# Splitting on GpSimd, and PSUM sums sorted by SyncE's DMAs, in a three-way attention loop

## The reference

```python
att = softmax(einsum('bthd,bshd->bhts', q * HD ** -0.5, k), axis=-1)
o = einsum('bhts,bshd->bthd', att, v)
```

## Time and profile before

| | us |
|---|---|
| median of 3 runs | 1794.24 |
| lowest, highest | 1793.36, 1794.6 |
| the profiled execution, by the same clock | 1795.07 |
| its span, first to last instruction | 1793.2 |
| TensorE matmuls, busy | 1589.7 (89%) |
| VectorE, busy | 1276.4 (71%) |
| ScalarE, busy | 1208.4 (67%) |
| GpSimd, busy | 697.1 (39%) |

### The profile page before, as it was taken

How to read it: one execution, slowest core, us unless ns; L and a number is a source line. 1 busy time by engine, 2 the same in 40 slices (tenths; PEclk the granted TensorE clock), 3 DMA queues, 4 the chain that set the end, 5 groups by cost and what they waited for, 6 DMA issues and landing times. The chain is left out here.

```text
span 1793.2 us, 36960 instructions
## 1 busy us (share of the span) xinstructions
PE 1589.7 (89%) x9638; PEld 728.6 (41%) x9638; DVE 1276.4 (71%) x3087; ACT 1208.4 (67%) x2377; POOL 697.1 (39%) x673
## 2 busy tenths in 40 slices
PE   3669947889999999999999999999999999855998
PEld 1217933333344343434434344334434343211665
DVE  6986856378787877878787787878787787452442
ACT  3325741757878778787878878787888878714333
POOL 7823441234344344344344334434434433221442
PEclk9559965889999999999999999999999999957999
DMA  2211125354564555465456456456455545030122
GB/s 51 73 44 37 47 54 71 42 80 62 63 77 65 66 71 77 53 78 73 56 71 78 65 60 85 59 64 77 64 67 71 76 50 72 2 36 26 58 60 58
DMA packets 132338, 109.25 MB, mean 61 GB/s; under 512 B 21824, under 2 KB 125248, under 8 KB 132288
## 3 DMA queue, kind: packets, MB, share of 16 engines
q1 hardware_dynamic: 130240, 104.44, 41.5%
q0 software_dynamic: 2048, 4.20, 0.9%
HBM read 19.26 MB, written 8.39 MB: 15 GB/s over the span
## 5 line engine op out<-in xcount | busy, mean ns | idle before, releaser
L1034 ACT ACTIVATE probs<-psum 128x512 f32<-128x512 f32 (+3 forms) x1536 | 737.8, 551 | 268.3 <-PE psum L1143 158.4
L915 DVE TENSOR_REDUCE mx_S<-psum 128x1 f32<-128x512 f32 x512 | 323.5, 684 | 74.6 <-PE psum L1128 72.7
L915 DVE TENSOR_REDUCE mx_C<-psum 128x1 f32<-128x512 f32 x512 | 317.5, 683 | 53.0 <-PE psum L1128 51.6
L915 DVE TENSOR_REDUCE mx_T<-psum 128x1 f32<-128x128 f32 (+3 forms) x512 | 240.6, 488 | 119.7 <-PE psum L1131 107.6
L847 POOL TENSOR_TENSOR rem_q<-f_q,parts_q 128x512 f32<-128x512 f32 x48 | 55.4, 1155 | 495.8 <-ACT parts_q L1020 479.2
L1128 PE MATMUL psum<-ks_S,qs_S 96*128 96x512 bf16 x512 | 201.7, 400 | 18.0 <-DMA ks_S<-parts_k 13.7
L1128 PE MATMUL psum<-ks_C,qs_C 96*128 96x512 bf16 x512 | 203.0, 398 | 12.4 <-DMA ks_C<-parts_k 7.3
L1143 PE MATMUL psum<-qs_C,ks_C 99*128 99x512 bf16 x512 | 193.6, 389 | 18.1 <-ACT probs L1034 11.5
L1143 PE MATMUL psum<-qs_S,ks_S 99*128 99x512 bf16 x512 | 195.9, 384 | 1.6 <-ACT probs L1034 0.9
L1128 PE MATMUL psum<-ks_T,qs_T 96*128 96x128 bf16 (+3 forms) x512 | 157.6, 310 | 7.4 <-DMA ks_T<-parts_k 6.0
L1143 PE MATMUL psum<-qs_T,ks_T 99*128 99x256 bf16 (+3 forms) x512 | 153.6, 302 | 7.6 <-ACT probs L1034 6.4
(11 more groups left out here) (188 smaller groups left out, 2702.3 us busy)
## 6 DMA issues: line engine op xcount, KB each, us to landing
qs_S<-parts_q SPq DMA_DIRECT2D x96, 128.0 KB, 4.2
ks_S<-parts_k SPq DMA_DIRECT2D x96, 128.0 KB, 6.8
qs_T<-parts_q SPq DMA_DIRECT2D x96, 128.0 KB, 4.4
ks_T<-parts_k SPq DMA_DIRECT2D x96, 128.0 KB, 6.8
qs_C<-parts_q SPq DMA_DIRECT2D x96, 128.0 KB, 4.4
ks_C<-parts_k SPq DMA_DIRECT2D x96, 128.0 KB, 6.8
w_in_S<-in_s_in SPq DMA_DIRECT2D x16, 257.0 KB, 2.7
w_in_T<-in_t_in SPq DMA_DIRECT2D x16, 257.0 KB, 2.7
```

Source lines behind the costliest of these rows:

```text
L915: nc.vector.tensor_reduce(mx[kind][:, n:n + 1], psum[:, ring_place(kind, b, n, RL), 0:last_key], AX_X, ALU.max)\
L1034: nc.scalar.activation(probs[:, n // 4 % 2, n % 4, t0:T], psum[:, LOGITS + ring_place(kind, b, n, RC), t0:T], ACT.Exp, scale=SCALE).then_i ...
```

## The change

Three things change in `attend`; the embedding stage and the MLP lose only the columns `low` and `high`.

1. GpSimd writes all parts. For queries, then for keys, it rounds high, subtracts, rounds middle, subtracts, where ScalarE did the two roundings; and it makes the three parts of the maxima (`split_maxima`, first in each slot), where VectorE did. The reduction itself negates, and VectorE only copies the transposed maxima out of `desk`.
2. After each group ScalarE copies the bank once, plainly, into `group_0` or `group_1`. SyncE sorts the 16-partition halves with DMAs of 32 KB, four to a call: first sums into `s_all` (end of the slot), second sums into `s_all`, second values over `group_0`'s sums. GpSimd's two additions and VectorE's shuffle go. The product now needs the second values landed, and ScalarE's copy into `group_0` at step 28 needs the product of the finishing unit (as `u_all` did).
3. SyncE's order in a slot: rows of maxima, weights, six query DMAs as their parts come, three DMAs of the keys' high part, second sums, three DMAs of the keys' middle and low parts, second values, and at the end first sums. The logarithm moves from step 21 to step 23 and reads `s_all`.

The diff of these places (indentation cut):

```diff
 TURN_AT, NEGATE_AT = 1, 1
 PROJECT_AT = (3, 7, 10)
-HIGH_AT, MIDDLE_AT = (4, 8), (9, 13)
+KEPT_AT = (4, 8)
 WEIGH_AT = 3
 VALUES_AT = 13
 GROUP_1_AT, GROUP_2_AT = 28, 12
-SWAP_AT, RECIP_AT = 17, 21
+RECIP_AT = 23
 OUTPUT_AT, KEEP_AT = 29, 31
 PROJECT_PARTS, OUTPUT_PARTS = (1, 1, 4), 2
 LAG = 8
...
     e = sp.value_load(expert[0:1, bass.ds(2 * b, 1)], min_val=0, max_val=K - 1)
     sp.dma_start(w_fold[:], folds[:, bass.ds(e, 1), :].rearrange("p o n -> p (o n)")).then_inc(fold_in, 16)
-def stack(kind, b):
+def stack(kind, b, c, which):
     if exists(b):
-        if not isinstance(b, int) or b >= 1:
+        tile, order = ((qs[kind], Q_PARTS), (ks[kind], K_PARTS))[c]
+        if c == 0 and (not isinstance(b, int) or b >= 1):
             sp.wait_ge(logits_in, TILES * (unit_no(kind, b - 1) + 1))
-        for c, (tile, order) in enumerate(((qs[kind], Q_PARTS), (ks[kind], K_PARTS))):
-            sp.wait_ge(lo_done, 2 * unit_no(kind, b) + c + 1)
-            sp.wait_ge(mid_done, 2 * unit_no(kind, b) + c + 1)
+        for part in which:
+            sp.wait_ge((hi_done, mid_done, lo_done)[part], 2 * unit_no(kind, b) + c + 1)
             for g in range(NPROD):
-                sp.dma_start(tile[HD * g:HD * g + HD, :, :],
-                             parts[c][:, order[g], :]).then_inc(stack_in[kind], 16)
+                if order[g] == part:
+                    sp.dma_start(tile[HD * g:HD * g + HD, :, :],
+                                 parts[c][:, part, :]).then_inc(stack_in[kind], 16)
+def halves(to, to_at, source, at, done):
+    for j in range(4):
+        sp.dma_start(to[32 * j + to_at:32 * j + to_at + HD, :],
+                     source[32 * j + at:32 * j + at + HD, :]).then_inc(done, 16)
+def gather_first_sums(kind, b):
+    u = unit_no(kind, b)
+    sp.wait_ge(low_out, u + 1)
+    halves(s_all, 0, group_0, HD, sums_0_in)
+def gather_second_sums(kind, b):
+    u = unit_no(kind, b)
+    sp.wait_ge(high_out, u + 1)
+    halves(s_all, HD, group_1, 0, sums_1_in)
+def gather_second_values(kind, b):
+    u = unit_no(kind, b)
+    sp.wait_ge(sums_0_in, 64 * u + 64)
+    halves(group_0, HD, group_1, HD, values_1_in)
 def slot_program(i, slot):
-    (kn, bn), _, (kb, bb), _ = units(i, slot)
+    (kn, bn), _, (kb, bb), (ko, bo) = units(i, slot)
     if exists(bb):
-        sp.wait_ge(neg_step, 5 * (unit_no(kb, bb) + 1))
+        sp.wait_ge(neg_step, 4 * (unit_no(kb, bb) + 1))
         for k in range(NPART):
             sp.dma_start(qs[kb][RA + k:RA + k + 1, :, :].rearrange("o h (n t) -> o (h n) t", t=P),
                          ng_p[:, k, :]).then_inc(rows_in[kb], 16)
...
         weights("T", i + 1, w_in["T"], t_in, win_in["T"], "vT")
         weights("T", i, w_out["T"], t_out, wout_in, "oT")
         fold(i)
-    stack(kn, bn)
+    stack(kn, bn, 0, (0, 1, 2))
+    stack(kn, bn, 1, (0,))
+    if exists(bo):
+        gather_second_sums(ko, bo)
+    stack(kn, bn, 1, (1, 2))
+    if exists(bo):
+        gather_second_values(ko, bo)
+    if exists(bb):
+        gather_first_sums(kb, bb)
 weights("S", 0, w_in["S"], s_in, win_in["S"], "vS")
 weights("T", 0, w_in["T"], t_in, win_in["T"], "vT")
 for tile, source in ((w_in["C"], c_in), (w_out["C"], c_out), (ob, c_bias)):
     sp.dma_start(tile[:], source).then_inc(w_fixed, 16)
 sp.dma_start(s_outs[:], s_out.rearrange("k p n -> p k n")).then_inc(s_outs_in, 16)
-stack("S", 0)
+stack("S", 0, 0, (0, 1, 2))
+stack("S", 0, 1, (0, 1, 2))
 sp.wait_ge(fold_kept, 2)
 whole_loop(sp, slot_program)
...
         return
     for c in range(2):
         n = 2 * unit_no(kind, b) + c
+        pool.wait_ge(desk_free, desk_use("qk"[c] + kind, b) + 1)
+        if before(kind, b):
+            pk, pb = before(kind, b)
+            pool.wait_ge(stack_in[pk], 16 * 2 * NPROD * (pb + 1))
+        pool.sem_inc(split_seen, 1)
+        nc.gpsimd.tensor_copy(parts[c][:, 0, :], f32[c][:]).then_inc(hi_done, 1)
         pool.wait_ge(hi_done, n + 1)
-        at_least(pool, mid_done, n - 1)
         nc.gpsimd.tensor_tensor(rem[c][:], f32[c][:], parts[c][:, 0, :], ALU.subtract)\
             .then_inc(rem_done, 1)
-    for c in range(2):
-        pool.wait_ge(mid_done, 2 * unit_no(kind, b) + c + 1)
+        pool.wait_ge(rem_done, n + 1)
+        pool.sem_inc(split_seen, 1)
+        nc.gpsimd.tensor_copy(parts[c][:, 1, :], rem[c][:]).then_inc(mid_done, 1)
+        pool.wait_ge(mid_done, n + 1)
         nc.gpsimd.tensor_tensor(parts[c][:, 2, :], rem[c][:], parts[c][:, 1, :], ALU.subtract)\
             .then_inc(lo_done, 1)
+def split_maxima(kind, b):
+    u = unit_no(kind, b)
+    pool.wait_ge(desk_free, desk_use("m" + kind, b) + 1)
+    if before(kind, b):
+        pk, pb = before(kind, b)
+        pool.wait_ge(rows_in[pk], 16 * NPART * (pb + 1))
+    pool.sem_inc(maxima_seen, 1)
+    nc.gpsimd.tensor_copy(ng_p[:, 0, :], ng[:]).then_inc(neg_step, 1)
+    pool.wait_ge(neg_step, 4 * u + 1)
+    nc.gpsimd.tensor_tensor(ng_r[:], ng[:], ng_p[:, 0, :], ALU.subtract).then_inc(neg_step, 1)
+    pool.wait_ge(neg_step, 4 * u + 2)
+    pool.sem_inc(maxima_seen, 1)
+    nc.gpsimd.tensor_copy(ng_p[:, 1, :], ng_r[:]).then_inc(neg_step, 1)
+    pool.wait_ge(neg_step, 4 * u + 3)
+    nc.gpsimd.tensor_tensor(ng_p[:, 2, :], ng_r[:], ng_p[:, 1, :], ALU.subtract).then_inc(neg_step, 1)
 def slot_program(i, slot):
-    (kn, bn), _, _, (ko, bo) = units(i, slot)
+    (kn, bn), _, (kb, bb), (ko, bo) = units(i, slot)
+    if exists(bb):
+        split_maxima(kb, bb)
     split(kn, bn)
-    if exists(bo):
-        u = unit_no(ko, bo)
-        pool.wait_ge(high_out, u + 1)
-        pool.wait_ge(low_out, u + 1)
-        nc.gpsimd.tensor_tensor(s_all[:], s_all[:], s_high[:], ALU.add).then_inc(s_merged, 1)
-        nc.gpsimd.tensor_tensor(u_all[:], u_all[:], u_high[:], ALU.add).then_inc(u_merged, 1)
     if slot == 0 and exists(i - 1):
         if not isinstance(i, int) or i >= 2:
             pool.wait_ge(desk_free, desk_use("oT", i - 2) + 1)
...
     if exists(bo):
         u = unit_no(ko, bo)
         pool.wait_ge(recip, u + 1)
-        pool.wait_ge(u_merged, u + 1)
+        pool.wait_ge(values_1_in, 64 * u + 64)
         if ko == "S":
             if not isinstance(bo, int) or bo >= 1:
                 pool.wait_ge(desk_full, desk_use("qC", bo - 1) + 1)
         elif before_in_oT(ko, bo):
             pool.wait_ge(desk_full, desk_use("o" + before_in_oT(ko, bo)[0], before_in_oT(ko, bo)[1]) + 1)
-        nc.gpsimd.tensor_tensor((oT_S if ko == "S" else oT)[:], u_all[:], s_recip[:], ALU.mult)\
+        nc.gpsimd.tensor_tensor((oT_S if ko == "S" else oT)[:], group_0[:], s_recip[:], ALU.mult)\
             .then_inc(o_ready, 1)
     if slot == 1 and exists(i + 1):
         pool.wait_ge(desk_full, desk_use("vS", i) + 1)
...
     u = unit_no(kind, b)
     dve.wait_ge(scored, TILES * u + n + 1)
     last_key = P * (n % NB + 1) if kind == "T" else T
-    nc.vector.tensor_reduce(mx[kind][:, n:n + 1], psum[:, ring_place(kind, b, n, RL), 0:last_key], AX_X, ALU.max)\
-        .then_inc(reduced, 1)
+    nc.vector.tensor_reduce(mx[kind][:, n:n + 1], psum[:, ring_place(kind, b, n, RL), 0:last_key], AX_X, ALU.max,
+                            negate=True).then_inc(reduced, 1)
 def negate(kind, b):
     u = unit_no(kind, b)
     dve.wait_ge(desk_full, desk_use("m" + kind, b) + 1)
-    nc.vector.tensor_scalar(ng[:], desk[0:TILES, 0:P], -1.0, None, ALU.mult).then_inc(desk_free, 1)
-    dve.wait_ge(desk_free, desk_use("m" + kind, b) + 1)
     if before(kind, b):
-        pk, pb = before(kind, b)
-        dve.wait_ge(rows_in[pk], 16 * NPART * (pb + 1))
-    nc.vector.tensor_copy(ng_p[:, 0, :], ng[:]).then_inc(neg_step, 1)
-    dve.wait_ge(neg_step, 5 * u + 1)
-    nc.vector.tensor_tensor(ng_r[:], ng[:], ng_p[:, 0, :], ALU.subtract).then_inc(neg_step, 1)
-    dve.wait_ge(neg_step, 5 * u + 2)
-    nc.vector.tensor_copy(ng_p[:, 1, :], ng_r[:]).then_inc(neg_step, 1)
-    dve.wait_ge(neg_step, 5 * u + 3)
-    nc.vector.tensor_tensor(ng_p[:, 2, :], ng_r[:], ng_p[:, 1, :], ALU.subtract).then_inc(neg_step, 2)
+        dve.wait_ge(neg_step, 4 * u)
+    nc.vector.tensor_copy(ng[:], desk[0:TILES, 0:P]).then_inc(desk_free, 1)
 def values(kind, b):
...
     shift = w_fold[:, P:P + 1] if kind == "C" and c == 0 else w_in[kind][:, W_BQ + c:W_BQ + c + 1]
     nc.scalar.activation(f32[c][:], desk, ACT.Identity, bias=shift)\
         .then_inc(desk_free, 1)
-    act.wait_ge(desk_free, desk_use("qk"[c] + kind, b) + 1)
-    if before(kind, b):
-        pk, pb = before(kind, b)
-        act.wait_ge(stack_in[pk], 16 * 2 * NPROD * (pb + 1))
-    nc.scalar.activation(parts[c][:, 0, :], f32[c][:], ACT.Copy).then_inc(hi_done, 1)
-def middle(kind, b, c):
-    if not exists(b):
-        return
-    act.wait_ge(rem_done, 2 * unit_no(kind, b) + c + 1)
-    nc.scalar.activation(parts[c][:, 1, :], rem[c][:], ACT.Copy).then_inc(mid_done, 1)
 def exponential(kind, b, n):
     u = unit_no(kind, b)
...
 def second_group(kind, b):
     u = unit_no(kind, b)
     act.wait_ge(summed, 8 * u + 8)
```

(19 more changed lines are left out.)

38 lines of the change are left out of this document (9 added, 29 removed).

## The result

The changed kernel takes 1955.37 us (median of 4 runs, 1949.12 to 1958.59) against 1794.33 us: 1.0893 times the time before, 95% interval 1.0878 to 1.0907. The forecast was 1910 us in a range of 1790 to 1965. Direction and place are right, the size is 161 us where 116 were worked out.

What follows compares the result with a forecast made beforehand. TensorE was taken as nearly the bound, with 2.7 us idle a turn. The forecast was 1795.07 + 103 (late moves) + 15 (clock) - 3 (gain in the last slots) = 1910 us, range 1790 to 1965.

Steps and rivals of the forecast that it cites:

- The bound and the ceiling: Loop turn: TensorE nearly the bound, 2.7 us idle, so relieving VectorE and ScalarE gains at most 40 us.
- GpSimd: Slot's start: eight GpSimd operations, some 9.5 us, cost nothing; rows of maxima come 0.75 us later, barely hidden.
- The start of the stack: SyncE's first stack DMA: f+6.05 in slot 1, f+3.5 in slot 0, some f+3.1 in slot 2.
- The line: SyncE's DMA queue: small moves stand behind stack DMAs of 1.06 us, taking 0.2 us each; 103 us in 15 turns.
- rival 1: DMA queue: small moves aren't late, sums land about 4.5 us after issue begins; 1755 us, chance 0.17.
- Which wait binds: Slot ends: late values delay the output projection 4.05 and 1.8 us (slots 1, 0), slot 2's logits 1.0; sum 6.85.
- The clock: TensorE after idle stretches: half clock could lose up to 3.5 us a turn; 1 us taken, 15 us in all.
- Rival 3: All slots: moves late and the clock falls in most turns, 133 + 52 us; 1980 us, chance 0.04.
- Signs: Changed trace: ScalarE idle 2 to 3 us before slot 1's logarithm, TensorE before output projection; DMA share over 0.54, turns 85-88 us.
- Rivals 1 and 2: Moves not late (1755 us, chance 0.17); or late only in slot 1, paid by gains elsewhere (1795 us, 0.09).

Runs made afterwards that it cites:

- Part 1 alone: Kernel before, with only GpSimd writing all parts of queries, keys and maxima, and sorting of sums and values as before: 1761.03 us, ratio 0.9814.
- half-stack run: Changed kernel, each stack DMA copying only the first 256 of 512 columns from the second sequence on: 1812.15 us, ratio 1.0072 to the kernel before.

## Why the prediction was right or wrong

**The bound and the ceiling: right, in part by luck.** TensorE had 2.7 idle us a turn, so relief was worth at most 40 us. Part 1 alone gave 35, but only half of it by the idle time of the steady turns; 15 us came in the first turns, which the sum doesn't look at. In the changed kernel some of the relief is there too, hidden under the stops: the wait of 0.64 us for the keys at 908.94 has gone, and so has this one, before the logits in slot 0:

```profile
921.45 0.39 PE L1143 MATMUL psum<-qs_C,ks_C 99*128 99x512 bf16 x1 [0.53 <-ACT probs L1034]
```

**GpSimd: right.** Its roundings of 512 columns take 0.61 us, inside the bounds of 0.20 and 1.16 (the upper end was taken), and the four operations on the maxima 0.28, 0.41, 0.28 and 0.42. The rows of maxima are issued 0.68 us later (forecast 0.75; at f-0.11 in slot 1, where the earlier trace rows have f-0.79) and landed before step 8.

```profile
L890 POOL CAST ng_p<-ng 32x128 bf16<-32x128 f32 x48 | 13.4, 280 | 284.0 <-DVE ng L965 284.0
...
L877 POOL CAST parts_k<-rem_k 128x512 bf16<-128x512 f32 x48 | 29.3, 609 | 8.0 <-POOL rem_k L873 8.0
```

**The start of the stack: right.** f+6.15, f+3.5 and f+3.3 in slots 1, 0 and 2, forecast 6.05, 3.5 and 3.1.

**The line: right, but not the landing of a move in it.** The half-stack run shows that the line is made of the stack's bytes, and the ninth stack DMA landed 11.85 us after the stack's start (forecast 11.8). The move was sized at 0.2 us. That is what it costs the line: the twelfth stack DMA landed 15.8 us and the last value 16.5 us after the start (forecast 15.8 and 16.6). But the sums landed 0.5 us apart, since the stack DMAs behind were served beside them. So they landed at f+19.9 in slot 1 (forecast 18.6), and the logarithm started at f+16.3 in slot 0 (17.1 in the next turn's) and f+17.4 in slot 2, where the forecast has 16.1 and 15.7. It was also asked for earlier than the one time that was worked out, f+15.7 in slot 1: at f+14.6 in slot 0 and f+14.9 in slot 2. (Moves that land 1.9 us after their issue are rival 1; the prediction once calls them the second rival.)

**Which wait binds: wrong.** The sum took the values' lateness as each slot's cost (4.05, 1.8 and 1.0 us) and the logarithm's as the smaller one behind it. In the trace TensorE stops at the third logits after the logarithm, for 4.54, 1.85 and 2.03 us, and 0.58 us more in slot 2 for the product. That is 9.0 us. The waits that went, and shorter ones, take off 1.9, so the idle time of a turn grew by 7.1 us, where 6.85 were worked out. That this is so close is in part luck, since the wait was the wrong one in slots 0 and 1 and the relief was left out. The rest is that both waits hang in the same line and are of nearly one size. In slot 1 the output projection could have started at f+24.1 (forecast 24.2), but TensorE was later than that. In slot 2, where the 0.58 us come last, the logits of step 31 start at f+22.5 (forecast 22.4). And with the sums ahead of the keys the values bind, and little is won.

**The clock: the failed step.** It was put at 1 us a turn because "much of the slow work would fall into waits" and the full stop was only in slot 1. It was 3.8 us a turn, 57 us instead of 15. The work after the stop is dense, TensorE is the bound there, and nothing takes up the loss; and stops near 2 us in slots 0 and 2 often brought it too. The earlier trace rows had shown half clock around a stop of only 1.42 us; it had begun ahead of that stop, since the slow matmuls there start at 348.02. With 57 in place of 15 the forecast would have been 1795.07 + 103 + 57 - 3 = 1952 us, against 1955. Rival 3, the clock falling in most turns, is what happened; its 52 us for the clock were right, its 133 for the waits too much. Its argument against itself, that only slot 1 has a full stop, didn't hold.

**Signs.** ScalarE's wait for the second sums and the product's for the values came as listed, but TensorE didn't stop before the output projection, the DMA share was 0.53 and not above 0.54, and the turn was 90.7 us, not 85 to 88.

**Rivals 1 and 2: excluded.** A full queue doesn't let a small move pass, nor does a second queue, and all three slots lose. Both orders that take the moves out from behind the keys (1804 and 1778 us) bring the time near to what rival 1 assumed.
